# A graph network's relation MLP on one Trainium2 core: at the odd octets the transposes of a later octet stand between the second-layer products and the last first-layer pair

## The reference, cut to what matters

```python
he = edge_features @ edge_fc_W + edge_fc_b
t = relu(einsum('ed,mdf->emf', he, rel_att_W1) + rel_att_b1[None])      # M = 3
g = sigmoid(einsum('emf,mf->em', t, rel_att_W2) + rel_att_b2[None])
beta = _seg_softmax(g, dst, n)
```

## Time and profile before

| | us |
|---|---|
| median of 3 runs | 2567.0 (2566.91 to 2568.18) |
| the profiled execution's own time | 2568.5 |
| span of its trace | 2566.9 |
| PE busy over the span | 2112.0 (82%) |
| DVE busy | 1811.4 (71%) |
| POOL busy | 1658.5 (65%) |
| ACT busy | 1533.1 (60%) |

### The profile page before, as it was taken

The page is one execution under the profiler, slowest core; times in us unless marked ns, Lnnn a source line. Parts: engine busy times, 40 slices in busy tenths (PEclk is TensorE's granted clock), DMA queues, the critical chain, the costliest instruction groups (busy, mean ns, idle before and its releaser), DMA issues. The chain is left out here.

```text
span 2566.9 us, 63030 instructions
## 1 busy us (share of the span) xinstructions
PE 2112.0 (82%) x16604; PEld 1421.1 (55%) x16604; DVE 1811.4 (71%) x6215; ACT 1533.1 (60%) x4445; POOL 1658.5 (65%) x1800
## 2 busy tenths in 40 slices
PE   5799999997999999999995757777777777777773
PEld 4333333332677777777775446556555555555551
DVE  7984556110788888888876548787888887878764
ACT  2466777776666777667762136666666666666641
POOL 1277777776777777777720057777777777777740
PEclk9999999999899999999997558898989888989885
DMA  9244444553777777777731022222222222222220
GB/s 94 60 142 131 132 132 133 150 141 96 213 202 197 202 203 201 201 201 202 200 102 35 28 62 80 79 78 79 79 79 79 79 78 79 79 78 78 79 50 25
DMA packets 213904, 297.98 MB, mean 116 GB/s; under 512 B 87552, under 2 KB 136597, under 8 KB 213808
## 3 DMA queue, kind: packets, MB, share of 16 engines
q0 software_dynamic: 78400, 180.35, 25.9%
q1 hardware_dynamic: 135408, 116.54, 17.9%
HBM read 238.46 MB, written 58.28 MB: 116 GB/s over the span
## 5 line engine op out<-in xcount | busy, mean ns | idle before, releaser
L1569 POOL DMA_INDIRECT sum_acc<-kv_table,rec_all x784 | 741.4, 946 | 239.1 <-issue 236.6
L1068 POOL DMA_INDIRECT area_b<-h_table,src_g x448 | 459.1, 1025 | 144.0 <-issue 126.6
L512 POOL DMA_INDIRECT early<-h_table,src_g x336 | 331.3, 986 | 222.2 <-ACT sum_acc L727 141.8
L727 ACT ACTIVATE sum_acc<-twin,bias 128x1024 f32<-128x1024 f32 x294 | 318.1, 1118 | 154.9 <-PE twin L597 151.1
L1655 ACT COPY sum_acc<-sum_acc 128x768 f32 x220 | 183.4, 833 | 307.6 <-POOLq L1575 189.5
L597 PE MATMUL twin<-area_b,wc 64*128 64x512 f32 x1176 | 313.6, 634 | 11.0 <-ACT sum_acc L727 11.0
L1141 PE MATMUL bank<-hs,y_sb 128*128 128x129 f32 x2344 | 311.2, 275 | 0.6 <-ACT y_sb L1164 0.6
L1141 PEld LDWEIGHTS bank<-hs,y_sb 128*128 128x128 f32 x2344 | 285.7, 192 | 1.3 <-ACT y_sb L1164 1.1
L1168 ACT COPY y_sb<-bank 128x512 f32<-128x512 f32 x293 | 171.8, 586 | 190.6 <-PE bank L1132 190.6
L1627 PE MATMUL twin<-sum_acc,probT 128*128 128x193 f32 x880 | 206.9, 387 | 27.5 <-DVE probT L1765 27.0
L1627 PE MATMUL bank<-sum_acc,probT 128*128 128x193 f32 x880 | 206.0, 385 | 25.0 <-DVE probT L1765 23.4
(11 more groups left out here) (311 smaller groups left out, 4685.5 us busy)
## 6 DMA issues: line engine op xcount, KB each, us to landing
hs<-rows_table SPq DMA_DIRECT2D x293, 258.0 KB
rows_table<-area_b POOLq DMA_DIRECT2D x112, 258.0 KB
area_b<-in_edge_attr SPq DMA_DIRECT2D x97, 256.0 KB, 2.9
rows_table<-early POOLq DMA_DIRECT2D x84, 258.0 KB
sum_acc<-kv_table,rec_all POOLq DMA_INDIRECT x784
area_b<-h_table,src_g POOLq DMA_INDIRECT x448
early<-h_table,src_g POOLq DMA_INDIRECT x336
kv_table<-sum_acc SPq DMA_DIRECT2D x25, 96.0 KB, 1.6
```

The costliest lines, as they stand in the source:

```text
L512: pool.indirect_dma_start(out=early[:, g % RINGE, j, 0:D], out_offset=None, in_=h_table, in_offset=bass.IndirectOffsetOnAxis(ap=src_g[:, g ...
L727: act.activation(hid_words[:, first:first + 2 * GE], twin[p % 2][:, :], ACT.Relu, bias=bias1[:, m:m + 1]).then_inc(hid_sb, 1)
L1068: pool.indirect_dma_start(out=landed_rows[:, g % RINGE * GT + j, 0:D], out_offset=None, in_=h_table, in_offset=bass.IndirectOffsetOnAxis(a ...
L1569: pool.indirect_dma_start(out=landed_rows[:, g % RING1 * GT + j, :], out_offset=None, in_=kv_table, in_offset=bass.IndirectOffsetOnAxis(ap ...
```

## The change

In the programs of PE and ACT the turn of octet o+3 and its copy stand at the same place in every octet. For even octets nothing changes. For odd ones `turn(o + 3)` moves from behind `hidden(o + 1, 2)` to before it, right behind `logits(o)`, and `turned(o + 3)` on ACT from behind the last ReLU to before it. It concerns the odd octets 1 to 93, 47 of them.

```diff
@@ the order on PE
                         if o % 2:
                             logits(o)
-                        elif o + 3 < OCTS:
+                        if o + 3 < OCTS:
                             turn(o + 3)
                         if o + 1 < OCTS:
                             hidden(o + 1, 2)
-                        if o % 2 and o + 3 < OCTS:
-                            turn(o + 3)
                         if o >= TILE and o % TILE == 0:
                             turn_logits(o // TILE - 1)
@@ the order on ACT
                         if o + 1 < OCTS:
                             rectified(o + 1, (0, 1))
-                        if o % 2 == 0 and o + 3 < OCTS:
+                        if o + 3 < OCTS:
                             turned(o + 3)
                         if o + 1 < OCTS:
                             rectified(o + 1, (2,))
-                        if o % 2 and o + 3 < OCTS:
-                            turned(o + 3)
                         if o >= TILE and o % TILE == 0:
                             gates(o // TILE - 1)
```

## The result

| | before | after |
|---|---|---|
| median, us | 2566.95 (2564.96 to 2568.18, 6 runs) | 2577.84 (2576.64 to 2580.72, 6 runs) |
| span of the profiled execution | 2566.9 | 2575.0 |
| start of the first logits to the start of the last (L608) | 514.9 (109.01 to 623.94) | 526.5 (108.52 to 635.04) |
| first work of the next block | 636.84 | 646.89 |

The changed kernel is 1.0044 times as long as the one before (95% interval 1.0031 to 1.0057), 10.9 us by the medians. The forecast was +11.2 and 2578.2 (2572 to 2583).

What follows compares the result with a forecast made beforehand. PE was taken to bound the relation MLP, its holes included. 12.8 us after the first fifteen octets, less 0.7 there and 0.9 caught up by POOL, made +11.2 us: 2578.2 on the median, range 2572 to 2583.

Steps and rivals of the forecast that it cites:

- The round trip of 2.39 us: From an octet's third first-layer product, through its ReLU on ACT, to the next octet's second, against 1.92 of PE work.
- The ordinary pair: Two octets, logits to logits, with nothing else in the gap: +0.44 us, 10.34 becomes 10.78.
- ACT before h2 at no cost: Copy moved ahead of the ReLU of h2, an octet's third first-layer product, into ACT's idle 2.45 us: cost 0, no gain.
- the turned logits: Six pairs with this work behind the even octet: PE's existing waits partly absorb the delay, +0.12, bounds 0 and 0.47.
- Sort transposes behind the odd octet cost 0: At 8 odd octets the sort's transposes, 1.0 us, stand between h2 and h0 and cover the round trip: cost 0.
- The other eight pairs at +0.47: Seven pairs with sort transposes behind the even octet, one with the plan's products: +0.37 and +0.10 each.
- The wait for DVE and its clock, -0.7: First fifteen octets: delay fills the 1.91 us wait at octet 14, leaving 0.9; full clock returns 1.64.
- POOL catches up 0.9: Stage's end: POOL's row gathers recover 2 x 0.44 of the delay in the last two changed pairs, bounds 0 and 3.1.
- Later stages as long as before: Stages after the relation MLP: unchanged length, with 2 us each way allowed for clock changes after a shifted start.
- The run of three that holds: Rival: three first-layer pairs join without waiting, saving 0.20 per pair, 2560.6 us; needs h2-to-h1 of 1.92 or less; 4%.
- The delay hidden by POOL: Rival: POOL's own pace, 9.6 us per ordinary pair, sets the stage's end, giving 2567 to 2570; 7%.
- Holes that cost clock: Rival: 4 to 8 of some 80 PE holes each drop the clock, adding 6 to 13 us, 2584 to 2591; 6%.

Runs made afterwards that it cites:

- PE's half alone: Kernel before with the turn moved before the third first-layer product on PE, ACT's copy left behind the last ReLU: 2586.32 us against 2570.97, ratio 1.0063.
- half ReLUs: ReLUs over 512 of 1024 columns, in the kernel before (2555.66 us, ratio 0.9943) and in the changed kernel (2558.53 us, ratio 0.9954).
- Ten runs: Kernel before with the two products that wait for DVE's counts one octet later, behind octet 15 instead of 14: 2564.59 us against 2566.81, ratio 0.9993.

## Why the prediction was right, point by point

- **PE is the bound of this stage and passes its holes on.** Right. The last logits come 11.6 us later, counted from the first; the next block starts 10.5 later on the same count.
- **The round trip of 2.39 us.** Right: 2.37 in both places. The ordinary pair was to be +0.44 and is +0.40 (10.34 to 10.74 as the mean); the 0.02 of the round trip counts in both holes. That makes 19 x 0.40 = 7.6 instead of 8.4. The wait for the ReLUs grew 2.5 times, from 11.0 to 27.3 us, where "about doubles" was said.
- **ACT before h2 at no cost.** Right for the ordinary pair (PE's half alone gave the same pair). That it "gains nothing either" was wrong in six places: at the turned logits it returns 0.49 each. PE's half alone costs 0.59 there (11.16 to 11.74), more than the upper bound of 0.47, and only the copy brings it down to the +0.10 measured. I had set +0.12, near its lower bound, for another reason, PE's own waits: that this number held is luck.
- **Sort transposes behind the odd octet cost 0.** Wrong by a little: +0.15 eight times (11.22 to 11.37), 1.2 us. The hole is covered as said, but a turn and the sort's transposes no longer touch, and in a row they take less, as the last section has it in numbers.
- **The other eight pairs at +0.47.** Right: +0.45 (10.86 to 11.32 behind even octets, 10.90 to 11.36 at the plan's products; the pair of octet 15 without its share of the clock).
- **The wait for DVE and its clock, -0.7.** Right in kind and short in size: between the first logits and those of octet 15 the kernel gained 1.11 us, and 0.2 more in the logits behind. The wait vanished altogether, only 0.4 of the delay came out behind it instead of 0.9, and the two products for the counts took 0.1 less (182.22 to 182.74 instead of 182.29 to 182.91).
- **POOL catches up 0.9.** Right: 3.13 became 2.23.
- **Later stages as long as before.** From the start of the second block to the end 1930.1 us before and 1928.1 after, in one execution each: nothing that could be told from the spread of the traces (last section).
- **Rivals.** The run of three that holds: not here, but real at a shorter round trip, under 1.82 and not under 1.92. The delay hidden by POOL: no, POOL waited 10 us longer. Holes that cost clock: no, 1.00 from 187.4 to 636, and in the whole stage PE waits 74 times for a ReLU, up to 0.4 each.
The sum by what was measured: 7.6 + 3.6 (eight at 0.45) + 0.5 (five at 0.10) + 1.2 - 1.3 (the wait and its clock) = 11.6, as counted; less 0.9 of POOL, 10.7. Two errors, 0.8 too much for the ordinary pairs and 1.2 too little for the sort's, nearly cancelled, together with the clock's 0.6. The mechanism was right; that the total came within 0.3 us of the medians' 10.9 is luck, the more so as the interval of the measurement alone is 8 to 15 us.

## What to carry to other kernels

With two buffers between PE and ACT, ask not how full each engine is but how long a buffer's round trip is (here 1.20 from PE's start to ACT's and 1.17 back), and what stands between a product and the one that reuses its buffer. Every other piece of work, a transpose or a second layer, is cover; spread it so that each round trip has one piece, and do not take one away because the engine behind it idles. A step moved into another engine's idle time costs nothing if what it works on is there by then: together with PE's turn the moved copy was free, without it it cost 0.85 a pair. It is mostly no gain either when the bound is elsewhere, and what it uncovers has to be paid.

## What the runs showed of the hardware that was not expected

- Transposes in a row are cheaper than parted ones. In the kernel before, the four of a turn take 0.49 us when the sort's eight follow, and the eight 0.97 behind them (211.45 to 211.94 to 212.91). In the changed kernel the four are followed by a first-layer pair and take 0.58 (rows 3 have the same), and the eight stand behind one and take 1.02 (233.19 to 234.21). Together that is the 0.15 of the prediction's miss. Before, around the eight at 211.94 that rows 5 show, then changed:

```profile
211.45 0.66 PE L586 MATMUL bank<-identf,area_b 128*128 128x128 f32 x4
...
212.91 1.99 PE L597 MATMUL twin<-area_b,wc 64*128 64x512 f32 x8
```

```profile
233.19 1.09 PE L625 MATMUL bank<-identf,area_b 128*128 128x128 f32 x8
234.21 1.99 PE L597 MATMUL twin<-area_b,wc 64*128 64x512 f32 x8
```

- A third joined pair of first-layer products costs 0.87 (2.79 for three), an unjoined one 1.06, and the view shows neither as idle time: with half ReLUs the runs of three took 3.00 us without a hole in the timeline. Only the starts tell them apart.
- Ten runs left a stage that is 3.8 us shorter in its trace unclear in the total (ratio 0.9993 [0.9984, 1.0003]). Where a part is shorter by less than the spread of the runs, the trace of the part is the better witness. The traces also say where the spread is: ordinary pairs of one kernel agree within 0.01 us, while the time from the next block's first work to the end, which no edit touches, is 1928.7 to 1934.6 us in the four traces taken on one chip.
